# Two-layer graph network: a turn's register load moved from in front of the scores to behind the projection

## Chip, cores, metric

The kernel runs on one core of a Trainium2 chip. The metric is the device time of one execution in microseconds, the median of three runs. The engines are TensorE (PE for its matmuls, PEld for its weight loads), VectorE (DVE), ScalarE (ACT), GpSimd (POOL) and SyncE (SP). A "q" behind a name (PEldq, ACTq) stands for the engine's sequencer: what it does itself, without the engine's data path.

## What is computed

6250 nodes with 256 features and 200,000 edges sorted by their target go through two layers. The first is an attention over the edges with 64 relations, an output projection and two normalisations. The change lies in the second:

```python
transformed = jnp.einsum('ni,rio->rno', x, W) + b[:, None, :]
msgs = transformed[edge_types, src]                     # one row per edge
agg = zeros((6, num_nodes, 256)).at[edge_types, dst].add(msgs)
s = transpose(agg, (1, 0, 2))                           # per node: 6 rows
q, k, v = split(s @ in_proj_w.T + in_proj_b, 3)         # 4 heads of 64
probs = softmax(einsum('nrhd,nshd->nhrs', q, k) / sqrt(hd))
attn = einsum('nhrs,nshd->nrhd', probs, v)
out = (mean_r(attn @ attn_out_w.T + attn_out_b) + x) @ proj_w.T + proj_b
```

and, after it, a layer norm of x plus that result. The sums `agg` run over six relations for each node; the attention is among the six sums of one node.

## The kernel before

Four phases run one after the other: `prepare_phase` (tables), `attend_phase` (first layer's attention), `update_phase` (its output, and the transformed rows `tx_rows` for the second layer) and `relate_mix_phase`, the one that is changed. It takes the last 2.7 ms of the span.

In this last phase a window is 21 nodes with six relation sums each, 126 rows, and a unit is 12 windows or 250 nodes (`SBW` = 12, `NU` = 25 units). Edges are taken in chunks of 128. GpSimd gathers the rows of `tx_rows` that a chunk names into one of 32 places of the ring `xg` (L1868). TensorE forms the chunk's sums by a matmul of a one-hot table with these rows (`sums`, L1913), VectorE adds them to the running accumulator (`add_sum`, L2261), and SyncE stores an accumulator row to memory once its window is complete (L1819). A chunk needs the place of its rows in the ring; these places are known from a table `place` only, so TensorE's sequencer reads them into registers (`places`, L1900), the six or seven values of a turn in one load.

The work is written out in turns (`turn`, one function per engine). A turn does the sums of 25/4 chunks, `LEAD` = 20 turns ahead, and one window of the attention. The first 20 turns (i is None) have sums only, and in the last four of them projections too; then each unit has turns x = 0 to 11. Units 1 to 22 are one loop body of the program; units 0, 23 and 24 are written out. The sums end with turn 3 of unit 23, so the last 20 turns have none. On TensorE a turn's order before the change is:

- `places` (L1900), the load of this turn's ring places;
- `scores` of this window (L1936 with the mask, L1944 with queries and keys), which waits for the exponentials of the window before;
- the first two sums (L1913);
- `weigh` (L1971), the shares of the window two turns back;
- in turns 3, 4 and 5 one of the three matrix products of the previous unit's nodes (`nodes`, L2004 to L2020);
- `queries_keys` (L1926), one projection of four matmuls, for a window four turns ahead;
- the third and fourth sum;
- in six of the turns the transposes of rows (`turn_rows`, L1959);
- `turn_shares` (L1978), which waits for ScalarE's copy of the shares (`copy_shares`, L2098);
- the remaining two or three sums;
- `gather` (L1989), which waits for ScalarE's copy L2104.

Each engine works through its own queue in the order written; between engines semaphores set the order. A sum waits for the VectorE addition three chunks back, since there are three PSUM banks. On VectorE a turn is: maxima of the scores (`maxima`, L2280, which waits for the scores), L2288, the reciprocals and shares of the window before (L2294, L2298), additions and new one-hot tables (L2251) for the turn's sums, and in some turns the nodes' steps. On ScalarE it is: copies of the weights `keep` for coming chunks (L2176), in turns 3, 5 to 9 and 11 one to three transfers, the exponentials (`exps`, L2077), `copy_shares`, the projection's copy (L2086), L2104 and the gather's copy L2111. In turn 9 ScalarE issues an input transfer and the two output transfers of the previous unit (L2155) ahead of the exponentials.

A register that a load has filled is held in the Python dictionary `at` until the sum that uses it is written out.

Of the kernel before, what the change touches and what calls it, by code (L numbers as in the profile page):

```python
# [39 lines left out]
SBW = 12  # L40
# [55 lines left out]
def past(i, n):  # L96

    return not isinstance(i, int) or i >= n
# [1530 lines left out]
def relate_mix_phase(nc, a, out, t):  # L1629

    with ExitStack() as ctx:
# [121 lines left out]
        def first_chunk(r):  # L1754

            return r * CHUNKS4 // 4
# [16 lines left out]
        def relating(k, r):  # L1773
            return not isinstance(k, int) or SBW * k + r < NV

        def chunks(k, r):

            if not relating(k, r):
                return []
            return [(k * CHUNKS + q, q) for q in range(first_chunk(r), first_chunk(r + 1))]  # L1780

        def another(i):
            return not (isinstance(i, int) and i >= NU - 1)

        def ahead(i, x):

            return (i, x + AHEAD) if x < SBW - AHEAD else (i + 1, x + AHEAD - SBW)

        with nc.Block() as block:
# [87 lines left out]
            def _(eng):  # L1877
# [19 lines left out]
                def places(k, todo):  # L1897

                    if todo:
                        regs = nc.values_load_multi_w_load_instructions(  # L1900
                            place[0:1, bass.ds(todo[0][0], len(todo))], engines=[mybir.EngineType.PE], min_val=0,
                            max_val=XR - 1, skip_runtime_bounds_check_because=why)[1]
                        for (c, q), reg in zip(todo, regs):
                            at[q] = reg

                def sums(k, c, q):

                    if q % 5 == 0:
                        eng.wait_ge(hot, k * (CHUNKS // 5) + q // 5 + 1)
                        eng.wait_ge(kept, k * (CHUNKS // 5) + q // 5 + 1)  # L1910
                    if past(c, BANKS):
                        eng.wait_ge(acc_done, c - BANKS + 1)
                    eng.matmul(p_a[q % BANKS][0:WR, 0:D], oh[:, q % OR, :],  # L1913
                               xg[:, bass.ds(at[q], 1), :].rearrange("p g c -> p (g c)"), start=True, stop=True
                               ).then_inc(summed, 1)

                def queries_keys(i, j):

                    c, piece = j % 4, j // 4
                    n = i * 12 + j  # L1920
                    if c == 0:
                        eng.wait_ge(xt_done, i * 6 + 2 * piece + 2)
                    if past(n, 1):
                        eng.wait_ge(qk_done, n)
                    for k in range(2):
                        mm = eng.matmul(p_q[:, 0:QP], wt[:, k, c, :], xt[piece][:, k, :],  # L1926
                                        start=(k == 0), stop=(k == 1))
                    mm.then_inc(qk_ps, 1)

                def scores(v, i, x):  # L1930

                    if past(v, 1):
                        eng.wait_ge(pr_done, v)
                    for e in range(2):

                        eng.matmul(p_sc[e][0:WR, 0:2 * WR], t.ident_b[0:WR, 0:WR], mask[:, :],  # L1936
                                   start=True, stop=False)
                    if x % 4 == 0:
                        eng.wait_ge(qk_done, i * 12 + x + 4)
                    at = slice(WR * x, WR * x + WR)  # L1940
                    for b in range(2):
                        for e in range(2):
                            rows = slice(HD * e, HD * e + HD)
                            mm = eng.matmul(p_sc[e][0:WR, WR * b:WR * b + WR], qk[rows, b, at],  # L1944
                                            qk[rows, 2 + b, at], start=False, stop=(b == 1))
                            if b == 1:
                                mm.then_inc(sc_ps, 1)

                def turn_rows(i, piece, k):

                    n = i * 6 + piece * 2 + k
                    if k == 0:
                        eng.wait_ge(st_in[piece], i * 16 + 16)
                    if past(n, 1):
                        eng.wait_ge(xt_done, n)
                    if piece == 0 and k == 0 and past(i, 2):
                        eng.wait_ge(g_done, i * 3 - 3)
                    for w in range(4):
                        mm = eng.transpose(p_row[:, WR * w:WR * w + WR], st[piece][:, w, P * k:P * k + P],  # L1959
                                           t.ident[0:WR, 0:WR])  # L1960
                    mm.then_inc(xt_ps, 1)
# [13 lines left out]
                def turn_shares(v):  # L1975

                    eng.wait_ge(shr_done, v + 1)
                    eng.transpose(p_m[0:WR, 0:P], shr[:, :], t.ident[:, :]).then_inc(gt_ps, 1)  # L1978
# [45 lines left out]

                def turn(k, r, i, x):
                    todo = chunks(k, r)
                    places(k, todo)
                    if i is None:
                        for c, q in todo:
                            sums(k, c, q)  # L2030
                        if x >= SBW - AHEAD:
                            queries_keys(*ahead(-1, x))
                        if x in TURNS and TURNS[x][0]:
                            turn_rows(0, *TURNS[x][1:])
                        return
                    v = i * SBW + x
                    scores(v, i, x)
                    for c, q in todo[0:2]:
                        sums(k, c, q)
                    if past(v, WEIGH):  # L2040
                        weigh(v - WEIGH, (x - WEIGH) % SBW)
                    if NODE <= x < NODE + 3 and past(i, 1):
                        eng.wait_ge(xt_done, i * 6 + 6)
                        nodes(i - 1, x - NODE)
                    if x < SBW - AHEAD or another(i):
                        queries_keys(*ahead(i, x))
                    for c, q in todo[2:4]:
                        sums(k, c, q)
                    if x in TURNS and (TURNS[x][0] == 0 or another(i)):
                        turn_rows(i + TURNS[x][0], *TURNS[x][1:])  # L2050
                    if past(v, WEIGH):
                        turn_shares(v - WEIGH)
                    for c, q in todo[4:]:
                        sums(k, c, q)
                    if past(v, GATHER):
                        gather(v - GATHER, i - (x < GATHER), (x - GATHER) % SBW)

                each(eng, turn)
                for v in range(NV, NV + GATHER):
                    if v - WEIGH < NV:  # L2060
# [421 lines left out]
```

## Time and profile before

| | us |
|---|---|
| median of three runs | 6843.11 |
| lowest and highest run | 6830.48, 6857.14 |
| span of the profiled execution | 5694.7 |
| median less this span | 1148.4 |
| last phase, from 3000 us to the end | 2695 |

The page gives no time of the profiled execution beyond its span. Its busy times are TensorE 86% of the span, VectorE 70%, GpSimd 61% and ScalarE 47%. In a list of groups or a timeline a line gives the source line, engine, operation, what is written and read with its shape, and a count; behind it stands the idle time of that engine just before, and what ended it. "issue" means that the engine waited for nothing that the profile shows. Ends of matmuls are modelled, so neighbouring matmuls overlap in the records.

### The profile page before, as it was taken

What the parts mean: (1) busy time and instruction counts of PE and PEld (TensorE: products, weight loads), DVE (VectorE), ACT (ScalarE), POOL (GpSimd) and SP (SyncE); (2) the same over time, 40 slices, a digit from 0 to 9 for tenths busy, and PEclk for the clock granted to TensorE, in tenths of its full rate; (3) what the DMA queues carried; (4) which work ended last, traced back from release to release, by engine and by line L of the source; (5) the groups of instructions that cost most, each with busy time, mean ns of one, the idle gap of its engine ahead of it and who ended that gap; (6) DMA issues with size and microseconds to landing.
All of it is one profiled execution on the core that took longest, in us unless ns stands there. A gap on an engine that the chain in (4) does not pass through costs nothing. (4 is left out here: it accounts for less than half of the span.)

```text
span 5694.7 us, 146960 instructions
## 1 busy us (share of the span) xinstructions
PE 4877.5 (86%) x41806; PEld 3603.8 (63%) x41807; DVE 3997.7 (70%) x12069; ACT 2701.6 (47%) x9241; POOL 3457.0 (61%) x3690
## 2 busy tenths in 40 slices
PE   8769988998888888867976888888888888888887
PEld 4358877887777778764534555555555556555554
DVE  6448888888888888866756666666666666666662
ACT  5446666666666666642211444434443444434344
POOL 4357777777777777763437755555565555655530
PEclk9879999999999999988988999999999999999998
DMA  6788888888888888895654544444444444444431
GB/s 204 147 248 244 253 249 249 253 251 250 252 249 251 250 251 247 241 169 152 223 187 140 154 136 126 131 134 124 140 130 126 137 131 130 136 121 128 132 93 32
DMA packets 559523, 1024.62 MB, mean 180 GB/s; under 512 B 83160, under 2 KB 345388, under 8 KB 559218
## 3 DMA queue, kind: packets, MB, share of 16 engines
q0 software_dynamic: 222096, 682.80, 42.4%
q1 hardware_dynamic: 209112, 190.72, 11.3%
q10 hardware_dynamic: 128074, 148.80, 8.9%
q14 instruction: 200, 1.64, 0.1%
q8 instruction: 41, 0.67, 0.0%
HBM read 883.11 MB, written 142.09 MB: 180 GB/s over the span
## 5 line engine op out<-in xcount | busy, mean ns | idle before, releaser
L1868 POOL DMA_INDIRECT rm_xg<-tx_rows,rm_src x1568 | 1492.3, 952 | 1002.8 <-PE rm_pa L1913 584.8
L936 POOL DMA_INDIRECT at_kv<-kv_rows,at_idx x1760 | 1675.3, 952 | 605.1 <-issue 477.1
L2261 DVE SCALAR_TENSOR_TENSOR rm_acc<-rm_acc,rm_kp,rm_pa 126x256 f32<-126x256 f32 x1875 | 898.4, 479 | 457.3 <-PE rm_pa L1913 340.4
L1913 PE MATMUL rm_pa<-rm_xg,rm_oh 128*126 x3750 | 1018.5, 398 | 71.4 <-ACT rm_kp L2176 36.6
L1913 PEld LDWEIGHTS rm_pa<-rm_xg,rm_oh 128*126 128x126 f32 x3750 | 656.9, 191 | 349.2 <-issue 251.4
L1044 PE MATMUL at_p_s<-at_hot,at_own 128*64 128x128 f32 x7040 | 732.4, 286 | 18.1 <-ACT at_own L1113 15.4
L1032 PE MATMUL at_p_k<-g_ident,at_kv 128*128 128x128 f32 x3520 | 482.6, 281 | 291.2 <-DMA at_kv<-kv_rows,at_idx 254.5
L1047 PE MATMUL at_p_s<-at_kt,at_own 128*64 128x128 f32 x7040 | 708.9, 279 | 0.0
L2077 ACT ACTIVATE rm_pr<-rm_psc,rm_ntop 126x126 f32<-126x126 f32 x1200 | 421.7, 364 | 590.1 <-DVE rm_ntop L2288 355.1
L1212 DVE SCALAR_TENSOR_TENSOR at_acc<-at_acc,at_fac,at_p_o 128x129 f32<-128x129 f32 x1760 | 612.4, 348 | 87.9 <-ACT at_fac L1126 38.3
L1113 ACT ACTIVATE at_own<-at_rec 128x256 f32 x1760 | 585.6, 406 | 127.6 <-issue 111.6
L1120 ACT ACTIVATE at_ex<-at_p_s,at_ntop 128x128 f32<-128x128 f32 x1760 | 500.3, 367 | 284.7 <-DVE at_ntop L1194 280.9
L1032 PEld LDWEIGHTS at_p_k<-g_ident,at_kv 128*128 128x128 f32 x3520 | 401.5, 144 | 332.0 <-issue 249.6
L1926 PE MATMUL rm_pq<-rm_xt,rm_wt 128*128 128x504 f32 x1200 | 587.5, 612 | 0.0
L1044 PEld LDWEIGHTS at_p_s<-at_hot,at_own 128*64 128x64 f32 x7040 | 441.7, 141 | 97.4 <-issue 89.1
L2280 DVE TENSOR_REDUCE rm_top<-rm_psc 126x2 f32<-126x252 f32 x600 | 223.8, 414 | 389.6 <-PE rm_psc L1944 316.9
L1064 PE MATMUL at_p_o<-at_kv,at_pt 128*64 128x129 f32 x7040 | 472.4, 276 | 8.3 <-DVE at_pt L1179 7.2
L1047 PEld LDWEIGHTS at_p_s<-at_kt,at_own 128*64 128x64 f32 x7040 | 466.8, 142 | 0.0
L1096 ACT ACTIVATE at_kt<-at_p_k,at_bk 128x512 f32<-128x512 f32 x440 | 303.6, 690 | 339.6 <-PE at_p_k L1032 200.9
L1186 DVE TENSOR_REDUCE at_cmax<-at_p_s 128x4 f32<-128x512 f32 x440 | 301.3, 685 | 220.9 <-PE at_p_s L1047 219.3
L1064 PEld LDWEIGHTS at_p_o<-at_kv,at_pt 128*64 128x64 f32 x7040 | 398.6, 138 | 28.9 <-issue 20.3
L2251 DVE TENSOR_SCALAR rm_oh<-g_iota,rm_rw 128x126 f32<-128x126 f32 x1875 | 404.0, 292 | 0.0
(307 smaller groups left out, 6870.4 us busy)
## 6 DMA issues: line engine op xcount, KB each, us to landing
at_row<-rows ACTq DMA_DIRECT2D x440, 128.0 KB
agg_rows<-rm_acc SPq DMA_DIRECT2D x300, 126.0 KB
rm_st<-agg_rows ACTq DMA_DIRECT2D x75, 504.0 KB
rm_srow<-agg_rows ACTq DMA_DIRECT2D x75, 504.0 KB
tx_rows<-up_tx SPq DMA_DIRECT2D x49, 768.0 KB, 3.6
at_kv<-kv_rows,at_idx POOLq DMA_INDIRECT x1760
rm_xg<-tx_rows,rm_src POOLq DMA_INDIRECT x1568
sums<-at_acc SPq DMA_DIRECT2D x196, 64.5 KB
```

Source lines behind the costliest of these rows:

```text
L936: eng.indirect_dma_start(out=kv[j][:, c, 16:16 + KV], out_offset=None, in_=t.kv, in_offset=bass.IndirectOffsetOnAxis(ap=idx[:, o:o + 1], a ...
L1032: mm = eng.transpose(p_k[k][:, c * P:c * P + P], kv[j][:, c, KAT + P * k:KAT + P * k + P], t.ident[:, :])
L1044: eng.matmul(p_s[j % 2][64 * k:64 * k + 64, at], own[:, o, P + 64 * k:P + 64 * k + 64], hot[j % 2][:, at], start=True, stop=False)
L1047: mm = eng.matmul(p_s[j % 2][64 * k:64 * k + 64, at], own[:, o, 64 * k:64 * k + 64], kt[j % 2][:, k, c, :], start=False, stop=True)
L1064: mm = eng.matmul(p_o[b][64 * k:64 * k + 64, VE * (c % 2):VE * (c % 2) + VE], pt[j % 2][:, c, 64 * k:64 * k + 64], kv[j][:, c, VAT[k]:VAT[ ...
L1113: ins = act(own[:, o, :], rec[:, bass.ds(held["slots"][k], 1), :].rearrange("p a c -> p (a c)"), ACT.Copy)
L1120: ins = act(ex[j % 4][:, c, :], p_s[j % 2][:, P * c:P * c + P], ACT.Exp, bias=ntop[j % 2][:, c:c + 1])
L1212: v.scalar_tensor_tensor(acc[:, o, :], acc[:, (o - 1) % ACCS, :], fac[j % 4][:, c:c + 1], p_o[c // 2][:, VE * (c % 2):VE * (c % 2) + VE], ...
L1868: eng.indirect_dma_start(out=xg[:, g % XR, :], out_offset=None, in_=t.tx, in_offset=bass.IndirectOffsetOnAxis(ap=of[:, g:g + 1], axis=0),) ...
L1913: eng.matmul(p_a[q % BANKS][0:WR, 0:D], oh[:, q % OR, :], xg[:, bass.ds(at[q], 1), :].rearrange("p g c -> p (g c)"), start=True, stop=True ...
L1926: mm = eng.matmul(p_q[:, 0:QP], wt[:, k, c, :], xt[piece][:, k, :], start=(k == 0), stop=(k == 1))
L2261: v_.scalar_tensor_tensor(acc[:, q % AR, :], acc[:, (q - 1) % AR, :], kp[0:WR, q % AR:q % AR + 1], p_a[q % BANKS][0:WR, 0:D], ALU.mult, AL ...
```

## The change

In the turns of a unit, `places` is called in front of the scores only in turn 0. In turns 0 to 10 it is called once more behind `queries_keys` and in front of the third sum, there for the chunks of the following turn. The 20 turns ahead of the first unit are as before. The values loaded, their number and the sums that use them stay the same. At turn 0 two loads are in one turn, at turn 11 none.

```diff
                 def turn(k, r, i, x):
                     todo = chunks(k, r)
-                    places(k, todo)
+                    if i is None or x == 0:
+                        places(k, todo)
                     if i is None:
                         for c, q in todo:
                             sums(k, c, q)
@@
                         nodes(i - 1, x - NODE)
                     if x < SBW - AHEAD or another(i):
                         queries_keys(*ahead(i, x))
+                    if x + 1 < SBW:
+                        places(k, chunks(k, r + 1))
                     for c, q in todo[2:4]:
                         sums(k, c, q)
                     if x in TURNS and (TURNS[x][0] == 0 or another(i)):
```

## Rows read from the trace of the kernel before

**Rows 1.** The page: busy us (share of the span) xinstructions of each engine

```profile
PE 4877.5 (86%) x41806; PEld 3603.8 (63%) x41807; DVE 3997.7 (70%) x12069; ACT 2701.6 (47%) x9241; POOL 3457.0 (61%) x3690
```

**Rows 2.** The steady stretch: us, busy PE, PEld, DVE, ACT, POOL, clock, DMA share, GB/s

```profile
3330.00:5590.00 2260.00, 1987.08 (x11652) 1316.59 (x11651) 1487.95 (x4832) 928.88 (x3647) 1263.76 (x1328) 0.99 0.44 127
```

**Rows 3.** Waits from 3121 to 5590: engine, line, waited for: us in total, times, longest

```profile
POOL rm_xg L1868 <- PE rm_pa L1913: 577.4, 554, 4.4
...
DVE rm_top L2280 <- PE rm_psc L1944: 269.4, 211, 7.1
PE rm_psc L1936 <- issue: 261.1, 277, 1.6
```

**Rows 4.** Line 1900, TensorE's sequencer: ns min/median/max, first and last start

```profile
L1900 PEldq TENSOR_LOAD <-rm_place x300: 1449/1582/2124, 2984.3 to 5534.1; - x150
```

**Rows 5.** Timeline of TensorE in one turn: start us, us, what, idle before

```profile
4513.70 0.57 PE L1989 MATMUL rm_pm<-rm_gt,rm_srow 126*128 126x84 f32 x4
4515.09 0.42 PE L1936 MATMUL rm_psc<-rm_mask,g_ident_b 126*126 126x252 bf16 x2 [0.81 <-issue]
...
4516.07 1.13 PE L1913 MATMUL rm_pa<-rm_xg,rm_oh 128*126 x4
...
4517.49 1.96 PE L1926 MATMUL rm_pq<-rm_xt,rm_wt 128*128 128x504 f32 x4
4519.28 1.03 PE L1913 MATMUL rm_pa<-rm_xg,rm_oh 128*126 x4
```

**Rows 6.** Line 1900 from 4504 to 4515, the loads of two turns

```profile
L1900 PEldq TENSOR_LOAD <-rm_place x2: 1562/1564/1567, 4504.3 to 4513.5; - x2
```

**Rows 7.** TensorE's waits inside one unit, from 4356 to 4459

```profile
PE rm_psc L1936 <- issue: 11.2, 11, 1.4
```

**Rows 8.** Timeline of TensorE, the start of turn 0 of that unit

```profile
4355.03 0.42 PE L1936 MATMUL rm_psc<-rm_mask,g_ident_b 126*126 126x252 bf16 x2 [1.40 <-issue]
```

**Rows 9.** Timeline of TensorE in one of the last turns, without sums

```profile
5603.58 0.68 PE L1989 MATMUL rm_pm<-rm_gt,rm_srow 126*128 126x84 f32 x4 [0.85 <-ACT rm_gt L2104]
5604.09 0.38 PE L1936 MATMUL rm_psc<-rm_mask,g_ident_b 126*126 126x252 bf16 x2
```

**Rows 10.** Line 1913 at 4516.1, the sequencer's preparation of the third sum

```profile
L1913 PEldq FUSED_REGOPS  x1: 46/46/46, 4516.1 to 4516.1; - x1
```

**Rows 11.** Timeline of TensorE ahead of the first unit, where a load follows L1926

```profile
3098.59 3.12 PE L1913 MATMUL rm_pa<-rm_xg,rm_oh 128*126 x12
3101.54 1.85 PE L1926 MATMUL rm_pq<-rm_xt,rm_wt 128*128 128x504 f32 x4
3103.23 1.03 PE L1913 MATMUL rm_pa<-rm_xg,rm_oh 128*126 x4
```

**Rows 12.** Line 1900 there, the load that belongs behind L1926 at 3101.54

```profile
L1900 PEldq TENSOR_LOAD <-rm_place x1: 1452/1452/1452, 3101.0 to 3101.0; - x1
```

**Rows 13.** Timeline of ScalarE in turns 8 and 9 (q is its queue's issue)

```profile
4431.58 0.29 ACT L2098 ACTIVATE rm_shr<-rm_pm 128x126 f32<-128x126 f32 x1
...
4433.98 0.31 ACT L2111 ACTIVATE rm_ut<-rm_pm 128x168 f32<-128x168 f32 x1 [1.03 <-PE rm_pm L1989]
...
4437.13 1.06 ACTq L2155 DMA_DIRECT2D out_dram<-rm_y  x2
...
4439.69 0.29 ACT L2098 ACTIVATE rm_shr<-rm_pm 128x126 f32<-128x126 f32 x1
```

**Rows 14.** Timeline of TensorE in turns 8 and 9 of that unit

```profile
4427.35 0.42 PE L1936 MATMUL rm_psc<-rm_mask,g_ident_b 126*126 126x252 bf16 x2 [0.61 <-issue]
...
4432.40 0.27 PE L1978 MATMUL rm_pm<-g_ident,rm_shr 128*126 128x128 f32 x1
...
4434.83 0.42 PE L1936 MATMUL rm_psc<-rm_mask,g_ident_b 126*126 126x252 bf16 x2 [0.88 <-issue]
...
4440.03 0.33 PE L1978 MATMUL rm_pm<-g_ident,rm_shr 128*126 128x128 f32 x1
```

**Rows 15.** Timeline of VectorE in turn 8

```profile
4429.23 0.73 DVE L2280 TENSOR_REDUCE rm_top<-rm_psc 126x2 f32<-126x252 f32 x2
```

## The prediction, made before the changed kernel was run

> **What bounds the kernel now.** I read the page first, then the busy times of the stretch in which the changed code repeats, then the waits there, then single turns. The page gives the span of 5694.7 us; the median of the runs is 6843.1 us, so 1148.4 us lie around the span. The profiled execution has no total of its own, so I take this remainder as fixed and apply the microseconds saved in the span to the median.
>
> The change touches only the last phase. In its steady stretch, 3330 to 5590, TensorE is busy for 1987 of 2260 us, VectorE 1488, ScalarE 929 and GpSimd 1264, at a granted clock of 0.99 [rows 1, 2]. TensorE is thus idle for 273 us, and between 3121 and 5590 it stood for 261.1 us in front of L1936, the first matmuls of `scores`, in 277 places, released by "issue", meaning no semaphore that the profile shows [rows 3]. Nearly all idle time of the bounding engine is this one hole, once per turn. The other engines wait for TensorE: GpSimd 577 us, VectorE 269 us in front of the maxima in 211 of the turns [rows 3].
>
> **The change, part by part.** Loads: 20 turns lie ahead of the first unit, then come 23 units with 12 turns each and 4 turns of the 24th, which makes the 300. The change leaves the 20 and the one at turn 0 of 24 units. It moves 23 x 11 + 3 = 256. Each keeps its address arithmetic (46 ns) and its load; nothing is added or dropped, and only TensorE's queue is touched.
>
> *Removed from in front of the scores.* The 277 holes sum to 261.1 us [rows 3]. In one unit the eleven moved ones are 11.2 us [rows 7], and the hole of turn 0, which stays, is longer than their mean, 1.40 us against 1.02 [rows 7, 8]. I take 1.2 us for each of 24, 28 us, and are left with 233 us for the moved ones. That is not all, since the hole is counted from the modelled end of the last gather matmul. The last 20 turns have no sums and so no load; there the gather's group runs from 5603.58 to 5604.26 and the scores start at 5604.09, 0.17 us before that end, with no idle time in front of them [rows 9]. So a turn without the load saves its hole plus 0.17 us of overlap: 256 x 0.17 = 43 us. Gross: 233 + 43 = 276 us, 1.08 us per moved load.
>
> *Added behind the projection.* Now the load stands behind the four matmuls of L1926, which last 1.96 us, and ahead of the third sum [rows 5]. What covers it is what is queued on TensorE when the sequencer gets there. The sequencer prepared the third sum, the very place where the load will be, at 4516.1, when TensorE was only starting on the first sum; the third sum's matmul ran at 4519.28 [rows 5, 10]. From 4516.1 a load of 1.6 us ends at 4517.7, one of seven values (up to 2.1 us) at 4518.2. The sum's weights have to be loaded one matmul of L1926 ahead of it, and these follow each other in (4519.28 - 4517.49) / 4 = 0.45 us, so the handover must be there by 4518.8. It fits with 0.6 us to spare in the worse case. The exact new order stands in this trace: ahead of the first unit, a turn's load follows straight on the previous turn's L1926. The load starts at 3101.0, 0.5 us before the L1926 group at 3101.54, and takes 1.45 us; the sums behind L1926 start at 3103.23 without idle time, like those of the turn before at 3098.59 [rows 11, 12]. The cover is the same group of matmuls as in every later turn. I cost the new place at 0. If that cover is missing, the cost is at most the load itself, 1.58 us plus 0.06 us; below zero it can't go, as nothing is removed there.
>
> The rows show that the scores were held until the load ended, that this load began only 0.2 us ahead of the gather's first matmul, and that the third sum was prepared three microseconds ahead of its run [rows 5, 6, 10]. The Trainium skill, "Perfetto Trace Analysis", section "Tensor Engine Instruction (MATMUL, LD_WEIGHTS)", puts the semaphore wait into a queue behind the sequencer, which is then free for the next instruction; by that alone the old load would have run well ahead of the gather's wait and its removal would bring nothing, the time of rival C. The late start at 4513.5 and the hole itself speak against it, and I give that reading no chance of its own. The Trainium skill, "TensorE: Matmul & The Clock Gate", table at its head, has a queue of 64 instructions for this engine, by which the cover in the new place would be safe, and the sum is the same.
>
> *Who waits behind it.* Queued behind the load are the third and fourth sum, the transposes, the shares' transpose, the last sums, the gather and the next scores. VectorE waits for the sums. It is not delayed as long as the load ends before L1926 does.
>
> *What is late next.* Taking about 1.08 us out of a turn brings the scores nearer to chains that start before them. (a) Turn 9. ScalarE copies the gather's result at 4433.98, then issues an input and two output transfers (4437.13 and 1.06 us on), only then runs the exponentials, and ends the shares' copy at 4439.69 + 0.29 = 4439.98; TensorE's L1978 waits for it and starts at 4440.03 [rows 13, 14]. This chain hangs on the gather of turn 8 and not on the scores, so turn 9 gives back all that it gained: its hole 0.88 + 0.17, some 1.0 us, x 23 = 23 us. (b) Turn 8. VectorE goes into the maxima at 4429.23 with no idle time, 1.88 us after the scores' start at 4427.35, so it is late already. The shares' copy ends at 4431.58 + 0.29 = 4431.87 and L1978 starts at 4432.40 [rows 13 to 15]. With 0.1 to 0.15 us for the signal and the weights, the slack is 0.4 us; the turn gains 0.61 + 0.17 and more in other units. Some 0.5 us is given back: 23 x 0.5 = 11 us. (c) All others have more room: VectorE waits 1.3 us for the scores in each of its 211 places [rows 3], and where it comes late, a sum two or three places on has slack. For all of them I set 4 us, between 0 and 30 (a further turn like 8 in each unit and a half of one more). (d) Turn 0 keeps its load; VectorE's late start there hangs on its own end of turn 11, so it moves along.
>
> GpSimd has 1264 + its issue gaps; its 577 us of waiting for TensorE are more than the 240 us taken out [rows 3]. The clock is at its full level but for 0.01 of the stretch [rows 2]; fewer holes give it no reason to fall. 0.
>
> Sum: 276 - 23 - 11 - 4 = 238 us. 6843.1 - 238 = 6605 us; the span would be 5457 us.
>
> **The rivals.**
> A, the forecast: the load vanishes under the projection, and turns 8 and 9 give theirs back: 6605 us. Its own range is 6565 to 6650, from no loss at all (6567) to twice the losses listed.
> B, another engine takes over in more turns. VectorE waits for the scores in 211 of 277 turns, so three turns a unit have no such wait, turn 0 and 8 and one more [rows 3]; turn 9 has ScalarE's transfers, and two or three more would have to be short of slack. If six turns of eleven keep only a fifth of the gain, 276 x (5/11 + 0.2 x 6/11) = 156 us are left: 6687 us. For it: VectorE's 1488 us of 2260 leave it little play once a turn has a microsecond less. Against it: its idle time of 772 us is over three times the saving.
> C, no effect: the load is exposed in the new place as it was in the old, because sums or semaphores hold the sequencer until L1926 is well under way. With about 1.1 us exposed per turn the sum is zero: 6843 us. Rows 10 to 12 speak against it.
> D, slower: the queue in front of the load drains. If the sequencer reaches it only when the last of L1926's four matmuls starts, 0.45 us of the 1.64 us are covered, 1.2 us are exposed, and the third sum restarts with its weights, some 0.2 us more. That is 1.4 against 1.08 saved: 256 x 0.32 = 82 us slower, 6925 us. It decides as soon as exposure passes 1.08 us, that is, when the load starts later than 0.6 us after L1926's first matmul. In the trace, its place is reached 1.4 us ahead of that matmul in the steady turn [rows 5, 10] and 0.5 us ahead in the first turns [rows 11, 12].
> E, more than the gross sum: nothing is given back, and the two mask matmuls go through in 0.38 us, as in the last turns, where they now take 0.42 [rows 5, 9]: 256 x 0.04 = 10 us more, 6557 us.
>
> **How the numbers follow.** A 0.66, B 0.22, C 0.04, D 0.03, E 0.05. The forecast is A's, 6605 us. The range should leave out C, D and the worse half of B: 6560 to 6700 us. The measurement tells about 0.5% from no change, 34 us here; A, B and E are all beyond it. Faster 0.93, same 0.04, slower 0.03.
>
> **What would show it.** The holes in front of L1936 should shrink to about 24 with 28 us, and in turns 1 to 11 the scores should overlap the gather's end. The load should stand at line 1900 300 times with its old duration, beginning ahead of L1926's matmuls, and no idle time of TensorE should stand in front of L1913 after L1926. A wait of some 1 us for the shares' copy should be new in front of L1978 in turn 9, and one of 0.3 to 0.6 us in turn 8. A unit should shrink by 238 / 23 = 10.3 us. Wrong would be: "issue" holes in front of L1913 or the transposes (C, D), VectorE's sums as TensorE's new releaser in many turns (B), or a lower granted clock.

## The result, and the profile after

| | before | after |
|---|---|---|
| median, us | 6839.2 | 6759.7 |
| lowest and highest, us | 6830.5, 6857.1 | 6748.9, 6771.3 |
| ratio, 95% interval | | 0.9885, 0.9861 to 0.9910 |

The change gains 79 us (1.15%). Forecast were 238 us and at least 143, so the time lies above the whole range. A second pair of measurements gives the same (a1: 6753.0 beside 6840.0, ratio 0.9886, 0.9848 to 0.9925).

The page of the changed kernel: its span, and its engines' busy time, span share and instructions.

```profile
span 6769.5 us, 146960 instructions
PE 5401.2 (80%) x41806; PEld 3832.3 (57%) x41807; DVE 4015.5 (59%) x12069; ACT 2681.7 (40%) x9241; POOL 3455.5 (51%) x3690
```

The first thing to see is the span. It is 6769.5 us and the run took 6771.3; the span of before was 5694.7 beside a median of 6843 [rows 1]. The kernel before, profiled again (b1), has a span of 6833.1 us in a run of 6834.9:

```profile
span 6833.1 us, 146960 instructions
PE 5393.4 (79%) x41806; PEld 3824.8 (56%) x41807; DVE 4024.3 (59%) x12069; ACT 2695.7 (39%) x9241; POOL 3462.4 (51%) x3690
```

So 1.8 us lie around a span. The 1148 us that the prediction put there are missing from its trace: that trace shows an execution unlike the timed ones. Most of them belong to the first layer, which the change doesn't touch. From 300 us to the first load of line 1900, then from there to the end, in the trace that the prediction read and in b1 (us, busy PE, PEld, DVE, ACT, POOL, clock, DMA share, GB/s):

```profile
300.00:2984.00 2684.00, 2316.16 (x27420) 1937.32 (x27419) 2096.78 (x5903) 1480.91 (x4654) 1829.37 (x1976) 0.96 0.81 236
2984.00:5694.00 2710.00, 2333.70 (x13450) 1540.59 (x13450) 1739.70 (x5639) 1067.37 (x4200) 1511.18 (x1588) 0.97 0.43 125
```

```profile
300.00:3887.00 3587.00, 2758.60 (x27625) 2143.88 (x27625) 2140.98 (x5965) 1511.21 (x4732) 1837.81 (x1983) 0.93 0.64 179
3887.00:6833.00 2946.00, 2447.21 (x13450) 1578.30 (x13450) 1740.68 (x5639) 1061.57 (x4200) 1514.13 (x1588) 0.94 0.40 115
```

The two stretches are 903 and 236 us longer in b1. VectorE, ScalarE and GpSimd are busy for nearly the same time in both traces, so they stand the longer. TensorE's matmul time grows too, by 442 and 114 us, at a granted clock of 0.93 and 0.94 in place of 0.96 and 0.97; how much of that growth is the clock isn't separated. One place shows it best: VectorE's maxima of the first layer, in the trace that was read and in b1 (busy us, mean ns, then idle time before them and what ended it).

```profile
L1186 DVE TENSOR_REDUCE at_cmax<-at_p_s 128x4 f32<-128x512 f32 x440 | 301.3, 685 | 220.9 <-PE at_p_s L1047 219.3 <-issue 0.6
```

```profile
L1186 DVE TENSOR_REDUCE at_cmax<-at_p_s 128x4 f32<-128x512 f32 x440 | 303.4, 690 | 894.7 <-DMA pre_rows_i<-pad_edge_type,pre_edge_i 849.8 <-PE at_p_s L1047 44.4 <-issue 0.5
```

They wait for L1047's matmuls in both. In b1 the idle time is four times as long, and the profile puts it down to a transfer of a phase long over. That name is wrong: what comes late is TensorE's own semaphore update. Set against the modelled ends of their matmuls, the recorded updates of L1047 come 0.02 us later at the median in the trace of before, and 3.2 us later in b1 and after. They come in bursts: the updates of some microseconds are held back, then all follow in order within tenths. With updates over 0.3 us late counted, and those less than 2 us apart taken as one burst, the last phase has 15 bursts per 100 us in b1 and 17 in the changed kernel, and none in the trace that the prediction read. VectorE's and ScalarE's own updates, where they are recorded, come about 0.01 us after the end at the median. Not all are: of VectorE's 4122 updates in the last phase b1 has a record of 3055, the trace that the prediction read of 4106, so the lateness is best read from the engine that waits, as below.

Here is one burst in the last phase of the changed kernel, on TensorE, VectorE and ScalarE (start us, us, what, idle before).

```profile
5381.47 0.71 PE L1944 MATMUL rm_psc<-rm_qk 64*126 64x126 f32 x8
...
5385.31 0.59 PE L1913 MATMUL rm_pa<-rm_xg,rm_oh 128*126 x2
5388.53 0.69 PE L1913 MATMUL rm_pa<-rm_xg,rm_oh 128*126 x2 [2.62 <-DVE rm_acc L2264]
```

```profile
5381.95 0.47 DVE L2264 SCALAR_TENSOR_TENSOR rm_acc<-rm_acc,rm_kp,rm_pa 126x256 f32<-126x256 f32 x1
5386.51 0.74 DVE L2283 TENSOR_REDUCE rm_top<-rm_psc 126x2 f32<-126x252 f32 x2 [4.08 <-remote]
```

```profile
5387.56 0.37 ACT L2080 ACTIVATE rm_pr<-rm_psc,rm_ntop 126x126 f32<-126x126 f32 x1 [4.78 <-DVE rm_ntop L2291]
```

The scores (L1944) end at 5382.18, and VectorE's maxima start at 5386.51, after 4.08 us of standing. TensorE runs on, until it has used up the three banks of the sums; then it stands for 2.62 us, for additions that VectorE could not make in time. This is how a late update comes back to TensorE.

The holes go as forecast, the other waits don't. TensorE's waits in the 264 turns from turn 12 to turn 275, in b1 and then in the changed kernel (us, times, longest):

```profile
PE rm_psc L1936 <- issue: 239.6, 259, 1.6
PE rm_pa L1913 <- DVE rm_acc L2261: 53.7, 65, 3.4
PE rm_pm L1978 <- ACT rm_shr L2098: 34.1, 30, 2.7
PE rm_pm L1989 <- ACT rm_gt L2104: 14.8, 6, 3.7
PE rm_pa L1913 <- issue: 10.4, 11, 2.7
PE rm_pm L1971 <- ACT rm_ut L2111: 6.4, 7, 1.8
```

```profile
PE rm_pa L1913 <- DVE rm_acc L2264: 100.5, 105, 3.3
PE rm_pm L1978 <- ACT rm_shr L2101: 53.8, 41, 2.8
PE rm_pm L1989 <- ACT rm_gt L2107: 38.7, 17, 5.1
PE rm_pm L1971 <- ACT rm_ut L2114: 37.0, 23, 3.7
PE rm_psc L1936 <- issue: 25.9, 21, 1.7
PE rm_pa L1913 <- issue: 23.9, 30, 2.1
```

The holes in front of L1936 fall from 239.6 to 25.9 us, as forecast. But the four waits for VectorE and ScalarE rise from 109 to 230 us, and the issue gaps elsewhere from some 14 to 45. Of 214 us taken out, about 59 leave TensorE's idle time. Its busy time falls by 12 us more (2114.9 to 2103.3), and the stretch shrinks by 70 us (2479.8 to 2409.6).

### The profile page after: what moved, and what is told of

It is laid out like the page before. It is cut to its first block and busy times, and to the rows that moved or that the text cites. A ratio compares the mean times of both kernels' runs of the same rounds, so it can differ in the third digit from the quotient of the medians.

```text
span 6769.5 us, 146960 instructions
## 1 busy us (share of the span) xinstructions
PE 5401.2 (80%) x41806; PEld 3832.3 (57%) x41807; DVE 4015.5 (59%) x12069; ACT 2681.7 (40%) x9241; POOL 3455.5 (51%) x3690
## 5 line engine op out<-in xcount | busy, mean ns | idle before, releaser
L1913 PE MATMUL rm_pa<-rm_xg,rm_oh 128*126 x3750 | 1112.0, 416 | 223.3 <-DVE rm_acc L2264 119.4
L1064 PE MATMUL at_p_o<-at_kv,at_pt 128*64 128x129 f32 x7040 | 710.1, 291 | 546.0 <-issue 456.2
L1913 PEld LDWEIGHTS rm_pa<-rm_xg,rm_oh 128*126 128x126 f32 x3750 | 661.3, 197 | 587.6 <-issue 497.0
L1064 PEld LDWEIGHTS at_p_o<-at_kv,at_pt 128*64 128x64 f32 x7040 | 474.8, 141 | 744.3 <-issue 730.4
L1044 PE MATMUL at_p_s<-at_hot,at_own 128*64 128x128 f32 x7040 | 772.1, 290 | 52.7 <-issue 50.5
L1047 PE MATMUL at_p_s<-at_kt,at_own 128*64 128x128 f32 x7040 | 753.2, 281 | 71.9 <-issue 71.4
L1926 PE MATMUL rm_pq<-rm_xt,rm_wt 128*128 128x504 f32 x1200 | 601.6, 625 | 0.0
L1032 PE MATMUL at_p_k<-g_ident,at_kv 128*128 128x128 f32 x3520 | 542.9, 304 | 48.5 <-issue 23.4
L1044 PEld LDWEIGHTS at_p_s<-at_hot,at_own 128*64 128x64 f32 x7040 | 460.4, 143 | 167.7 <-issue 165.3
L1047 PEld LDWEIGHTS at_p_s<-at_kt,at_own 128*64 128x64 f32 x7040 | 493.2, 143 | 90.8 <-issue 90.3
L1032 PEld LDWEIGHTS at_p_k<-g_ident,at_kv 128*128 128x128 f32 x3520 | 475.1, 160 | 55.4 <-issue 45.7
```

Source lines behind the costliest of these rows:

```text
L1032: mm = eng.transpose(p_k[k][:, c * P:c * P + P], kv[j][:, c, KAT + P * k:KAT + P * k + P], t.ident[:, :])
L1044: eng.matmul(p_s[j % 2][64 * k:64 * k + 64, at], own[:, o, P + 64 * k:P + 64 * k + 64], hot[j % 2][:, at], start=True, stop=False)
L1047: mm = eng.matmul(p_s[j % 2][64 * k:64 * k + 64, at], own[:, o, 64 * k:64 * k + 64], kt[j % 2][:, k, c, :], start=False, stop=True)
L1064: mm = eng.matmul(p_o[b][64 * k:64 * k + 64, VE * (c % 2):VE * (c % 2) + VE], pt[j % 2][:, c, 64 * k:64 * k + 64], kv[j][:, c, VAT[k]:VAT[ ...
L1913: eng.matmul(p_a[q % BANKS][0:WR, 0:D], oh[:, q % OR, :], xg[:, bass.ds(at[q], 1), :].rearrange("p g c -> p (g c)"), start=True, stop=True ...
```

## The experiments

The theory after this reading: the moved load costs nothing at its new place, and the forecast gain exists where TensorE's updates come in time; where they come late, the holes were also time in which VectorE and ScalarE caught up, so most of the gain is given back. The rivals: the prediction's turns 8 and 9 are worse than thought; or the load is exposed in its new place.

**Both kernels again.** No edit.

> The unchanged kernel of before, for a second trace of it. Two theories. (F) Something outside the changed lines stops the engines at random places in an ordinary execution, and the trace of before, whose span of 5694.7 us is 1148 us short of its own timed runs, is one execution in which it did not. Then this trace has a span near 6840 us, its first layer takes about 3900 us and not 2960, VectorE stands for some 900 us in it, and in the last phase VectorE stands 1 to 4 us in front of the maxima in many turns, with the holes in front of the scores still there. (G) The change itself made VectorE late: then this trace has a span near 5700 us again and VectorE waits in front of the maxima for the scores alone.

> The changed kernel unchanged, a second trace of it beside b1 on the same chip. (F) 80 us faster than b1 in the timed runs, and nearly all of it in the last phase; the same sort of random stops on VectorE and ScalarE as in b1, with a like sum, so that what the removed holes give is paid back where TensorE now waits for VectorE or ScalarE. (G) the stops stand in this kernel only.

Measured: 6839.9 us (ratio to before 0.9998, 0.9983 to 1.0012) and 6753.0. The 79 us stand.

**Some of the turns only.** Turns 1, 2, 3, 5, 7, 10 and 11 have the moved load in one kernel, and 4, 6, 8 and 9 in the other; the rest keep it in front of the scores.

```
-                    if i is None or x == 0:
+                    if i is None or x not in (1, 2, 3, 5, 7, 10, 11):
                         places(k, todo)
...
-                    if x + 1 < SBW:
+                    if x + 1 in (1, 2, 3, 5, 7, 10, 11):
                         places(k, chunks(k, r + 1))
```

> The load moved only for turns 1, 2, 3, 5, 7, 10 and 11, the ones with slack in the trace of before; turns 4, 6, 8 and 9 keep theirs in front of the scores. Their holes are 7.0 of the 10.2 us of a unit. (C, the loss sits in a few turns whose other engines are late already) this kernel is as fast as the changed one or faster, 80 us or more below before. (D, the loss is spread over all turns, since signals come late anywhere) it gains in the share of the holes, about 55 us.

> The complement: the load moved only for turns 4, 6, 8 and 9. (C) near 0 us gained, since turns 8 and 9 give all back and 4 and 6 most. (D) in the share of the holes, 3.2 of 10.2 us, about 25 us gained.

Measured: seven turns 6780.3 us, ratio 0.9918 (0.9898 to 0.9938), 54 us less; four turns 6799.1, ratio 0.9946 (0.9925 to 0.9966), 35 us less. Per turn that is 54 / (7 x 23) = 0.33 us and 35 / (4 x 23) = 0.38. The loss doesn't sit in 4, 6, 8 and 9: the other seven turns give no more for each. The parts, 54 and 35 us, add up to the whole within their intervals.

**A second load, front and back.** Reading the same places twice, in either position, came to nothing (6834.7 us, ratio 0.9999; 6762.6, ratio 0.9895): the trace has 300 loads in both, so the compiler had dropped the repeated one, and the runs are the two kernels again. The load was then split in two, the first two places in one and the other four or five in the other, in front of the scores in the kernel before and behind the projection in the changed one:

```
-                    places(k, todo)
+                    if i is not None and x > 0 and len(todo) > 2:
+                        places(k, todo[0:2])
+                        places(k, todo[2:])
+                    else:
+                        places(k, todo)
```

> The kernel before, with the load in front of each turn's scores split in two (the first two places in one load, the rest in another), in all turns of the units. A load stood 1449 ns at the median, so TensorE stands some 1.4 us more in each of 276 turns, 390 us in all. If TensorE's time is the run's time, as the prediction had it: about +380 us over the kernel before, 7220. If 1 us of a TensorE hole is worth only what the moved load gave back per us (79 of 276 us, a share of 0.29, because the rest comes back as waits for VectorE and ScalarE): about +110 us, 6950; a larger share, up to 0.6, would not surprise, since here TensorE's share of the time goes up and not down (7075).

> The changed kernel, with the load behind the projection split in two in the same way. If the new place is covered by the projection with 0.6 us to spare, as the prediction had it, the second load of 1.45 us opens a hole of some 0.85 us in 276 turns: +235 us over the changed kernel, 6995. If the cover is already gone in ordinary executions and each load there costs its whole time, +400 us, 7160. If a hole is worth a share of 0.29 only, and the cover holds: +70 us, 6830. Nothing to be seen (6760) would say that the sequencer runs far ahead of TensorE there.

Beside them, on the same chip, ran two more edits of the changed kernel: a projection matmul more in each turn, and ScalarE's transfers of turns 8 and 9 moved.

```
-                    for k in range(2):
+                    for k, last in ((0, True), (0, False), (1, True)):
                         mm = eng.matmul(p_q[:, 0:QP], wt[:, k, c, :], xt[piece][:, k, :],
-                                        start=(k == 0), stop=(k == 1))
+                                        start=(k == 0), stop=last)
```

> The changed kernel, with the first of the two projection matmuls of each turn done twice: 1.0 us (601.6 us by 600 matmuls) more of TensorE's busy time in each turn, 300 us in all, and only one more matmul's signal-free records. It leaves nothing out. If TensorE bounds the turns: +290 us, 7050. If TensorE's time is worth a share of 0.29: +87 us, 6847. It also gives the load more cover, which would make it a little cheaper still if the cover were short.

```
-                    if x == 8:
-                        load_nodes(i)
-                    if x == NODE + 6 and past(i, 1):
-                        store(i - 1)
                     exps(v, x)
                     if past(v, WEIGH):
                         copy_shares(v - WEIGH)
+                    if x == 8:
+                        load_nodes(i)
+                    if x == NODE + 6 and past(i, 1):
+                        store(i - 1)
```

> The changed kernel, with ScalarE's loading of the node rows (turn 8) and its store (turn 9) moved behind the exponentials and the copy of the shares. The prediction put 34 us of lost gain on turns 8 and 9, where ScalarE issues these transfers ahead of that work: if that is right, 25 to 35 us are gained, 6728. If the loss is spread over all turns, as the two halves of the turns together suggest, at most 10 us, 6750 to 6760.

On this chip the kernel before took 5709.4 us, not 6840, and the traces have next to no late update: L1047's come 0.02 us after the end at the median, and the last phase has one to three bursts in all. It is the condition of the trace that the prediction was made from. Front split: 5800.8 us, ratio 1.0164 (1.0149 to 1.018), 91 us slower. Back split: 5440.6, ratio 0.9524. One long: 5625.7, ratio 0.9857. Late issue: 5410.8, ratio 0.9479 (0.9466 to 0.9492). My sizing of the split was wrong: the median of 983 ns is that of the longer part, and the shorter takes about 520, so the sum is only 0.05 us over the whole load. With the gap of 0.15 us between the two, the holes in front of L1936 are 306 us in the stretch of 264 turns, in place of 252. The stretch grows by 76 us, more than the 54 of the holes: TensorE's clock stands at the lower of its levels, 1.2 GHz, for 99 us of it, in place of 41 in the kernel before, and the turns that this touches account for some 25 us more. Line 1900 in the kernel with the load split in front:

```profile
L1900 PEldq TENSOR_LOAD <-rm_place x556: 517/984/1869, 2991.4 to 5620.2; - x186
```

**The changed kernel there, and the edits under late updates.**

> The changed kernel, unchanged, once more, beside the kernel before. So far the kernel before has taken two times: about 6840 us, with TensorE's signals seen late in bursts (some 16 bursts per 100 us of the trace), and 5709 us, with next to none, like the trace that the prediction was made from. Theory: the change gives its forecast in the second condition and a third of it in the first. So, where the kernel before takes about 5709: 5709 less 238 by the prediction's sum, 5470, or less by what late_issue left (5411 there, so 5411 to 5445). Where it takes about 6840: 6755 again. A rival says that the change is worth 1.1 to 1.2% in either condition (5645).

> The changed kernel with ScalarE's transfers of turns 8 and 9 behind its exponentials and copy of the shares, now beside the changed kernel itself on one chip. By the prediction's terms it gives 25 to 35 us over the changed kernel where TensorE's signals come in time (5411 against 5445). If the loss there is spread over all turns: at most 10 us. Where they come late: 0 to 20 us (6740 to 6755).

> The kernel before with the load in front of the scores split in two. Where the signals come in time it was 92 us slower than the kernel before, with the two loads of 983 ns at the median in place of one of 1.45 us, so 0.5 us more of a hole in some 260 turns, 135 us: a share of 0.7. Where they come late, theory (a hole is worth a share of 0.3 there): 40 us slower, ratio 1.006. Rival (TensorE's time counts in full in both, and the changed kernel loses at its new place): 90 to 135 us slower, ratio 1.013 to 1.02.

> The changed kernel with the first projection matmul of each turn done twice; TensorE was 235 us longer busy in it where the signals came in time, and the run 215 us longer than late_issue's 5411. Where the signals come late, theory (TensorE's time is worth a third there, whatever is taken from or added to it): 70 to 80 us over the changed kernel, about the time of the kernel before, ratio 1.000. Rival (only holes are worth little there, since late signals stand beside them, but busy time counts in full): 215 us over, ratio 1.02.

> The changed kernel, unchanged, beside the kernel before. Where the kernel before takes about 5709 us (TensorE's signals in time): 5411 to 5445 by the theory, 5470 by the prediction's sum. Where it takes 6840 to 6910: some 76 us less.

In after_third the updates came late (before 6908.1): the changed kernel took 6837.3 us, ratio 0.9903 (0.9872 to 0.9933); two further pairs gave 0.9891 and 0.9883. After_sixth met the other condition: before 5701.2, changed 5440.6, ratio 0.9539 (0.9523 to 0.9556), 261 us less. The rival that the change is worth the same share everywhere has fallen. Each edit, in both conditions:

| edit | updates in time | updates late |
|---|---|---|
| the change, against before | -261 us | -79 us |
| load split in front, against before | +91 us | +28 us (1.0043, 1.0025 to 1.0061) |
| a projection matmul more, against the changed kernel | +185 us | +62 us |
| ScalarE's transfers behind, against the changed kernel | -30 us | +10 us (within the spread) |
| load split behind, against the changed kernel | 0 | not run |

(Of the middle column the last three rows compare medians measured on two chips, on which before took 5709.4 and 5701.2, so some 8 us of them are open. All other rows compare kernels measured together.) The first three edits do different things: one takes a hole away, one makes it longer, one adds busy time. Each is worth 0.30 to 0.34 as much where the updates come late, by the medians. The intervals are wide: the five pairs of before and changed kernel give 71 to 87 us, a share of about 0.3, and the split's 17 to 42 us are a fifth to a half of its 91. So it isn't the load's new place, and not holes alone: TensorE's time counts about a third there of what it counts where the updates come in time.

The traces suggest how. In the 264 turns, with 14 to 17 bursts per 100 us in each kernel of the third column, one trace for each number:

| kernel | in time, us | late, us | added, us |
|---|---|---|---|
| load split in front | 2376 | 2537 | 161 |
| before | 2300 | 2480 | 180 |
| one long | 2218 | 2446 | 228 |
| changed | 2047 | 2410 | 363 |
| late issue | 2011 | 2446 | 435 |

The late column has a spread: five traces of the changed kernel give 2390 to 2437. The less TensorE has to do or to stand for in a turn, the more the same bursts add. In b1, 98 of the 264 turns take at most 0.15 us more than the time of their kind with updates in time; in the changed kernel 58. The reading that fits is that a turn that was long because of the load absorbed part of a burst, VectorE and ScalarE making up their delay while TensorE's sequencer was loading. It is argued from these counts; no edit separates it. Nor are the bursts alone in the third column: TensorE's clock stands at its lower level for 181 us of the stretch in b1 and 184 in the changed kernel, against 41 and 7 with updates in time.

**The other engine's side.** VectorE's two maxima of each turn twice, the first time into tiles that nothing reads:

```
                     for e in range(2):
+                        v_.tensor_reduce(idle[x % 2][e][:, :],
+                                         p_sc[e][0:WR, 0:2 * WR].rearrange("p (b m) -> p b m", b=2),
+                                         AXX, ALU.max)
+                    for e in range(2):
```

> The changed kernel with VectorE's two maxima over the scores of each turn taken twice, the first time into tiles that nothing reads: 2 x 0.41 us, 0.83 us more in each of 276 turns, 229 us in all, in the chain scores, maxima, exponentials, shares. Theory (with TensorE's signals late, the two thirds of a TensorE hole that give no time back are taken over by this chain of VectorE and ScalarE): the chain's time counts for most of the rest there, 100 to 160 us over the changed kernel. Rival (late signals alone set the pace, a delay of VectorE's hides beside them as TensorE's does): 0 to 60 us. Where the signals come in time and TensorE is busy 89% of the time: 0 to 60 us.

It ran where the updates come in time: 5457.7 us beside the changed kernel's 5440.6, 17 us more, with VectorE 189 us longer busy (4173.8 against 3985.0). So a tenth of VectorE's work counts there. Under late updates it wasn't tried, and that the chain of VectorE and ScalarE holds the other two thirds is therefore argued from the waits and the table, not shown by an edit.

## Why the prediction was wrong, step by step

**The step that failed** is the first: the 1148.4 us "lie around the span", taken as fixed, and "the microseconds saved in the span" applied to the median. The runs have 1.8 us around the span. The Trainium skill, "Runtime: NRT & Kernel Launch", section "The ~15µs preamble/postamble breakdown", gives about 9 to 15 us around a kernel. The 1.8 us between time and span here lie below that; either figure would have told that 1148 us can't be there. So the trace was of an execution 17% shorter than those to be forecast, and the question should have been what lengthens them and what that does to the gain. No row of that trace showed a late update. What the mismatch called for was a case of its own, in which much of the gain is lost, reaching to near zero; rival B, with 156 us left, was built on short slack in six turns and still gives twice what was measured.

Against the execution that was read the working holds, and after_sixth tests it. TensorE's waits in its 264 turns, its loads, and one load and its neighbours (the whole of a turn 8):

```profile
PE rm_psc L1936 <- issue: 26.5, 22, 1.5
PE rm_pm L1978 <- ACT rm_shr L2101: 22.6, 23, 1.3
PE rm_pa L1913 <- DVE rm_acc L2264: 20.1, 22, 1.7
```

```profile
L1900 PEldq TENSOR_LOAD <-rm_place x300: 1449/1463/2220, 2980.8 to 5264.8; - x150
```

```profile
L1900 PEldq TENSOR_LOAD <-rm_place x1: 1453/1453/1453, 4288.8 to 4288.8; - x1
```

```profile
4287.72 0.38 PE L1936 MATMUL rm_psc<-rm_mask,g_ident_b 126*126 126x252 bf16 x2
4288.03 0.71 PE L1944 MATMUL rm_psc<-rm_qk 64*126 64x126 f32 x8
4288.66 1.13 PE L1913 MATMUL rm_pa<-rm_xg,rm_oh 128*126 x4
4289.72 0.42 PE L1971 MATMUL rm_pm<-rm_pr,rm_gd 126*32 126x126 f32 x8
4290.07 1.96 PE L1926 MATMUL rm_pq<-rm_xt,rm_wt 128*128 128x504 f32 x4
4291.87 1.35 PE L1913 MATMUL rm_pa<-rm_xg,rm_oh 128*126 x4
4293.05 0.27 PE L1978 MATMUL rm_pm<-g_ident,rm_shr 128*126 128x128 f32 x1
4293.16 1.22 PE L1913 MATMUL rm_pa<-rm_xg,rm_oh 128*126 x4
4294.22 0.57 PE L1989 MATMUL rm_pm<-rm_gt,rm_srow 126*128 126x84 f32 x4
```

The same stretch of 264 turns in before and in after_sixth, where the updates come in time (us, busy PE, PEld, DVE, ACT, POOL, clock, DMA share, GB/s):

```profile
3212.79:5512.44 2299.65, 2025.34 (x11837) 1344.60 (x11837) 1532.61 (x4975) 940.69 (x3696) 1342.26 (x1410) 0.99 0.45 131
```

```profile
3203.27:5250.42 2047.15, 1973.77 (x11836) 1321.99 (x11837) 1522.37 (x4973) 931.61 (x3696) 1346.83 (x1414) 1.00 0.51 147
```

- *Holes removed.* Forecast: only those of turn 0 stay, 28 us in 24. There are 26.5 us in 22 places, where the same stretch of before had 252 in 264. Right.
- *Overlap and mask matmuls.* 43 us by the sum, 10 more only in rival E. In every moved turn of the stretch the scores now start 0.16 us before the modelled end of the gather, 0.16 x 242 = 39 us, and the mask's two matmuls let the next ones start 0.045 us sooner, 11 us. The 11 belonged into the sum. (TensorE's busy time falls by 51 us, 2025 to 1974, but that is not these two alone: the clock, below, is in it, and some overlap is lost where new waits stand.)
- *The new place at 0.* The load starts at 4288.8, 1.3 us ahead of the projection, and ends at 4290.3, while L1926 runs to 4292.0; the third sum follows with no idle time. Over the moved loads it started 1.29 us ahead of the projection at the median and always ended before the projection did, by 0.77 us at the least. Even under late updates it did, by 0.3 us at the least in the changed kernel's trace. Cut in two it costs nothing there, and 91 us in front of the scores. Right; C and D are out in both conditions.
- *Turn 9 gives back 23 us.* TensorE's wait for the shares' copy is 22.6 us in 23 places, 22 of them in turn 9. Right, in place and size:

```profile
4297.96 1.06 ACTq L2158 DMA_DIRECT2D out_dram<-rm_y  x2
4299.15 0.37 ACT L2080 ACTIVATE rm_pr<-rm_psc,rm_ntop 126x126 f32<-126x126 f32 x1 [2.87 <-issue]
...
4300.53 0.29 ACT L2101 ACTIVATE rm_shr<-rm_pm 128x126 f32<-128x126 f32 x1
```

```profile
4300.87 0.33 PE L1978 MATMUL rm_pm<-g_ident,rm_shr 128*126 128x128 f32 x1 [1.06 <-ACT rm_shr L2101]
```

  With the transfers behind the exponentials (late_issue), turn 9 falls from 7.91 to 6.41 us, and 30 us of the time go.
- *Turn 8 gives back 11 us.* Right in size, wrong in what is waited for. No wait for the shares' copy is new: it runs at 4292.59, and L1978 follows at 4293.05 without idle time. But turn 8 does lose time. From its scores to the next ones it takes 6.9 us; with the hole and the overlap in front of the next scores taken out, it should take 6.4. The 0.54 us, 12 us in 22 units, sit in its sums: the third and fourth take 1.35 us and the next two 1.22, where the same groups of before took 1.03 each:

```profile
4431.54 1.03 PE L1913 MATMUL rm_pa<-rm_xg,rm_oh 128*126 x4
...
4432.51 1.03 PE L1913 MATMUL rm_pa<-rm_xg,rm_oh 128*126 x4
```

  VectorE, already late in this turn, now does its five additions one behind the other, and TensorE's sums follow them: the fourth and the sixth sum start 0.13 us after the end of an addition, 4292.52 after 4292.39 and 4293.69 after 4293.56. The gaps are under the 0.15 us from which a wait is listed, so no view of waits shows them. Here is VectorE in after_sixth, its timeline from 4290 to 4295:

```profile
4291.90 2.81 DVE L2264 SCALAR_TENSOR_TENSOR rm_acc<-rm_acc,rm_kp,rm_pa 126x256 f32<-126x256 f32 x5 [0.37 <-issue]
```

  It isn't ScalarE's transfer: in late_issue, where that stands behind the exponentials, turn 8 is as long (6.95 us against 6.94).
- *All others, 4 us.* Turn 7 gives back 3 us, the rest 1; L1913's listed waits for VectorE are 20.1 us, as before (19.7). Right.
- *The clock, 0.* Wrong. In this condition before ran 41 us of the 264 turns at the lower of TensorE's levels, 1.2 GHz, and the changed kernel 7; the late_issue and split-behind kernels none. The turns that the lower level touches cost some 16 us more in before than in the changed kernel. "Fewer holes give it no reason to fall" was right, but fewer holes also took away most of the falls that were there.
- *The whole.* Forecast 10.3 us for a unit; measured (2299.6 - 2047.2) / 22 = 11.5, and 10.8 over turns at the upper level in both traces. In the 22 units 275 us are removed, 38 come back (turn 9: 22, turn 8: 12, the others 4) and the clock gives 16, which makes the 252 measured. The forecast for 22 units was 228. So the terms that were missing are the 11 us of the mask and the 16 of the clock; what comes back is 38 us, where 36 were forecast. Forecast 238 us in all; measured 261.

So with updates in time the sum was 9% short. With updates late the term "what is late next" (38 us) is what is mis-sized: about 155 us return to TensorE as waits and gaps in the stretch alone, over all turns. The argument "ScalarE and VectorE idle for over three times the saving" looks at totals; that idle time stands ahead of a late update and can't be used after it. The clock has a part too. With updates late it is 0.96 in the stretch in b1 and in the changed kernel, so the 16 us that it gives back with updates in time are missing. They are among the 40 us by which TensorE's busy time falls short: it falls by 12 us there and by 51 with updates in time. The other 142 of the 182 us by which the stretch falls short (252 less 70) are TensorE's idle time.

## What to carry to other kernels

Compare the span with the run's time first; when they differ by more than a few microseconds, the trace isn't like the timed executions, and a sum made from it forecasts a condition that they aren't in. A hole of the bounding engine is also slack for all that wait for it: if something else delays their start now and then, filling the hole gives back only a part of it, and edits of three different kinds (hole out, hole longer, work added) tell that share, here about a third. Delays under the threshold of a list of waits show only as groups that got longer: compare each turn with what it should take. Behind that, a blocking register load belongs behind a long group of matmuls, where the sequencer gets to it early.

## What the runs showed of the hardware

- One program on one chip of this kind took 5701 to 5709 us or 6834 to 6917, by medians, and kept to the one or the other in all runs made together (lowest and highest 5696.2 and 5715.8; 6813.1 and 6936.6). What differs in the traces is the lateness of TensorE's semaphore updates: 0.02 us against 3.2 at the median in the first layer, in 14 to 17 bursts per 100 us in either phase, though TensorE has 15 matmul and weight records per us in one and 9 in the other. The late traces also hold fewer records of updates, 58,011 in b1 against 104,772 in the trace of before. The chip numbered 6 met both conditions, 6840 and 6834 us and later 5709; if that number is one and the same chip, it isn't the chip alone. Its cause stays open. More instruction fetching it isn't: the two instruction queues move 200 and 41 packets in before and in b1. The Trainium skill, "NOTIFIC — the notification-queue block", section "7.1 Overflow: three behaviours, one of which stalls the engine", says that the block which writes an engine's records out holds producers back rather than lose one inside it; whether an engine was held back so no run here tests, and that so many update records are missing says that the records themselves were not all kept.
- In such bursts the profile names a wrong releaser (a finished transfer, "remote"); a releaser of a phase long over is the sign to look for.
- A register load costs, at the shortest, 0.52 us for two values, 0.98 for four, 1.45 for six and 1.69 for seven: 0.23 us for each and some 0.05. The Trainium skill, "Runtime: NRT & Kernel Launch", section "Instruction fetch mechanics", has about 200 ns for a register in the loads at a launch; the traces are a little above it.
- Where TensorE stands less, its clock falls less: with updates in time the lower level took 99 us of the 264 turns with 306 us of holes, 41 with 252, 7 with 26, and none in late_issue, one_long and back_split.
